# Dispatching sixteen experts from GpSimd: unrolled, with indices read in place, four output buffers and gathers five experts ahead

## The chip, the cores and the metric

The kernel runs on one core of a Trainium2 chip. The time is the device time of one execution in microseconds (us). All runs shown are of one core, and the time is that of the whole program: two transformer layers, of which the change touches one stage.

## The reference

The input x is 2 x 1024 tokens of 128 numbers. Four blocks follow each other, each with a residual and a layer norm: an attention with its own scoring, a mixture of 16 experts, a softmax attention, and a mixture of 8 experts. The change lies in the second block. Cut to what matters there:

```python
E, D = 16, 128; I = 4 * D; C = int(T * 2.0 / E)           # T = 2048 tokens, so C = 256 an expert
logits = flat_x @ gate_w.T
scores = softmax(logits, axis=-1).T
topk_weight, topk_idx = top_k(scores, C)                  # each expert picks its 256 tokens
xg = flat_x[topk_idx]                                     # gather
g = einsum("ecd,eid->eci", xg, Wg); u = einsum("ecd,eid->eci", xg, Wu)
h = gelu(g) * u
eo = einsum("eci,edi->ecd", h, Wd) * topk_weight[..., None]
flat_out = zeros_like(flat_x).at[topk_idx.reshape(-1)].add(eo.reshape(-1, D))   # scatter-add
out = flat_out.reshape(b, s, d) + shared                  # shared: one dense gated layer for all tokens
```

A token can be picked by several experts, so scatters of different experts may add to the same row.

## The kernel before, in words

Each engine runs its own written-out list of instructions, and semaphores order them. Nothing is scheduled by a planner.

For the expert stage the token lists lie in the SBUF tile `idx` (128 partitions x 16 experts x 2 halves, NH = 2, so 256 tokens are two columns of 128). DRAM holds `xs_rows` (the tokens and their 16 scores, 144 numbers a row) and `moe_rows` (the output rows, already filled with residual and shared part). For each expert e = 4 * j + k:

- **GpSimd (POOL) gathers**: two indirect DMAs (L1967, one per half) copy the expert's 256 rows of `xs_rows` into `G[:, k]`. `G` has four buffers. Before this `gather` (L1963) copies the two index columns to `idx_in[:, k]`, and the DMAs read that copy.
- **TensorE (PE)** turns the tokens (L913), runs the two upward products (L925, `expert_up`) and the downward product (L935, `expert_down`) with weights that SyncE (SP) loads four experts ahead (`load_expert`, L569 and L570, issued as soon as the downward product of expert e is done, `down_full`).
- **ScalarE (ACT)** does the gelu (L1291). **VectorE (DVE)** copies the turned tokens to `GT` and increments `g_sb` (L1670), multiplies (L1677, `hidden`), and in `weigh` (L1685) writes the weighted output to `out_e[:, k % 2]`, of which there are two buffers, and increments `out_sb`. So it waits until the scatter of expert e - 2 has landed (`scattered`).
- **GpSimd scatters**: two indirect DMAs that add (L1983) from `out_e` to `moe_rows`, with an index copy of their own, `idx_out` (L1975). Since two scatters may meet on one row, scatter e waits until all of scatter e - 1 has landed (`scattered` at 32 * e), and until `out_sb` says e + 1.

GpSimd's list is in the order `ORDER`, once for experts 0 to 3, then in a loop over j = 1, 2 with register values in waits and indices, then the last four scatters:

```python
ORDER = [("g", 0), ("g", 1), ("s", 0), ("g", 2), ("s", 1), ("g", 3), ("s", 2), ("s", 3)]
```

"g", k gathers expert 4 * j + 4 + k. So between scatters 3 and 4 (7 and 8, and so on) lie two gathers, and none between 2 and 3 (6 and 7, 10 and 11). The tiny `carrier` addition (L1958, `carry_waits`) stands between the waits and the DMAs; it computes nothing that is used. `idx_ready` counts the index copies.

After the last scatter has landed SP loads `moe_rows` back into `Z` (L594) and the layer norm on DVE (L1528 and on) begins; everything later in the program follows from that. Ahead of the stage, GpSimd waits for the lists (`idx_sb`, written by DVE at L1658).

Of the kernel before, what the change touches and what calls it, by code (L numbers as in the profile page):

```python
# [28 lines left out]
F32 = mybir.dt.float32  # L29
BF16 = mybir.dt.bfloat16  # L30
F16 = mybir.dt.float16
I32 = mybir.dt.int32
U32 = mybir.dt.uint32
ALU = mybir.AluOpType
# [3 lines left out]
P = 128  # L38
# [102 lines left out]
E0 = 16  # L141
I0 = 4 * P
CAP = 2 * B * T // E0
NH = CAP // P
# [31 lines left out]
def build(nc, a, out):  # L176
    with ExitStack() as whole:
        def sem(name):
            return whole.enter_context(nc.semaphore(name))
# [4 lines left out]
        def sb(name, shape, dt, scope=whole):  # L184
            return scope.enter_context(nc.sbuf_tensor(name, shape, dt))
# [6 lines left out]
        xs_rows = dram("xs_rows", [B * T, XW], F32)  # L192
        moe_rows = dram("moe_rows", [B * T, P], F32)
# [8 lines left out]
        banks = [t[:, h * BANK:(h + 1) * BANK] for t in (causal_ps[0], causal_ps[1], tail_ps, acc_ps)  # L202
                 for h in range(2)]
# [10 lines left out]
        eps_ln = sb("eps_ln", [P, 1], F32)  # L214
# [120 lines left out]
        lists = sb("lists", [P, 2, 16], F32, M)  # L335
        turned_l = sb("turned_l", [P, 2, 2, 16, 8], F32, M)
        idx = sb("idx", [P, E0, NH], I32, M)
        carrier = sb("carrier", [P, 1], F32, M)
        idx_in = sb("idx_in", [P, 4, NH], I32, M)
        idx_out = sb("idx_out", [P, 4, NH], I32, M)  # L340
        G = sb("G", [P, 4, NH, XW], F32, M)
        w_tok = sb("w_tok", [P, 4, NH], F32, M)
        GT = sb("GT", [P, 2, CAP], F32, M)
# [2 lines left out]
        wd = sb("wd", [P, 4, I0], F32, M)  # L346
        act_e = sb("act_e", [P, 4, CAP], F32, M)
        hid_e = sb("hid_e", [P, 2, 4, CAP], F32, M)
        out_e = sb("out_e", [P, 2, NH, P], F32, M)
        M.close()  # L350

        N = ExitStack()
# [85 lines left out]
        hid_done = sem("hid_done")  # L438
        down_full = sem("down_full")
        out_sb = sem("out_sb")  # L440
        idx_ready = sem("idx_ready")
        scattered = sem("scattered")
        z_in = [sem(f"z_in{n}") for n in range(CH)]
        w2_in = sem("w2_in")
# [913 lines left out]
        def _(dve):  # L1358
# [320 lines left out]

            def weigh(j, k):  # L1680
                dve.wait_ge(down_full, 4 * j + k + 1)
                if k >= 2 or not isinstance(j, int) or j > 0:
                    dve.wait_ge(scattered, 16 * NH * (4 * j + k - 1))
                for h in range(NH):
                    ins = dve.tensor_scalar(out_e[:, k % 2, h, :], banks[6 + k % 2][:, h * P:(h + 1) * P],  # L1685
                                            w_tok[:, k, h:h + 1], None, ALU.mult)
                ins.then_inc(out_sb, 1)

# [168 lines left out]
        def _(pool):  # L1857
# [95 lines left out]
            pool.wait_ge(masks_ready, 3)  # L1953
            pool.nop().then_inc(masks_ready, 1)

            def carry_waits():

                pool.tensor_tensor(carrier[:, :], eps_ln[:, :], eps_ln[:, :], ALU.add)  # L1958

            def gather(e, k):  # L1960

                src = idx[:, e, :] if isinstance(e, int) else idx[:, bass.ds(e, 1), :].rearrange("p o h -> p (o h)")
                pool.tensor_copy(idx_in[:, k, :], src).then_inc(idx_ready, 1)  # L1963

            def fetch(k):
                for h in range(NH):
                    pool.indirect_dma_start(out=G[:, k, h, :], out_offset=None, in_=xs_rows,  # L1967
                                            in_offset=bass.IndirectOffsetOnAxis(ap=idx_in[:, k, h:h + 1].bitcast(U32), axis=0)
                                            ).then_inc(gathered[k], 16)

            def scatter(j, k):

                e = 4 * j + k
                src = idx[:, e, :] if isinstance(e, int) else idx[:, bass.ds(e, 1), :].rearrange("p o h -> p (o h)")
                pool.tensor_copy(idx_out[:, k, :], src).then_inc(idx_ready, 1)  # L1975
                pool.wait_ge(idx_ready, 4 + (8 * j if not isinstance(j, int) or j < 3 else 24) + scat_at(j, k))
                pool.wait_ge(out_sb, e + 1)

                if not (isinstance(e, int) and e == 0):
                    pool.wait_ge(scattered, 16 * NH * e)  # L1980
                carry_waits()
                for h in range(NH):
                    pool.indirect_dma_start(out=moe_rows, in_=out_e[:, k % 2, h, :], in_offset=None,  # L1983
                                            out_offset=bass.IndirectOffsetOnAxis(ap=idx_out[:, k, h:h + 1].bitcast(U32), axis=0),
                                            compute_op=ALU.add).then_inc(scattered, 16)

            ORDER = [("g", 0), ("g", 1), ("s", 0), ("g", 2), ("s", 1), ("g", 3), ("s", 2), ("s", 3)]

            def scat_at(j, k):

                order = ORDER if not isinstance(j, int) or j < 3 else [o for o in ORDER if o[0] == "s"]
                return order.index(("s", k)) + 1

            pool.wait_ge(idx_sb, 1)
            pool.wait_ge(xs_out, 16 * 2)
            for k in range(4):
                gather(k, k)
            pool.wait_ge(idx_ready, 4)  # L2000
            for k in range(4):
                fetch(k)
            pool.wait_ge(sh_out, 16 * CH)

            def four_experts(j):
                for n, (kind, k) in enumerate(ORDER):
                    if kind == "g":

                        pool.wait_ge(g_sb, 4 * j + k + 1)
                        gather(4 * j + 4 + k, k)  # L2010
                        pool.wait_ge(idx_ready, 4 + 8 * j + n + 1)
                        carry_waits()
                        fetch(k)
                    else:
                        scatter(j, k)

            four_experts(0)
            with pool.Fori(1, E0 // 4 - 1) as j:
                four_experts(j)
            for k in range(4):  # L2020
                scatter(E0 // 4 - 1, k)


            pool.wait_ge(w2_in, 16 * 6)
# [94 lines left out]
```

## Time and profile before

| | us |
|---|---|
| median of 3 runs | 1172.78 |
| lowest, highest of them | 1169.59, 1176.74 |
| the profiled execution's own time | 1178.61 |
| its span | 1176.9 |
| granted TensorE clock, mean over the span | 0.875 of full |
| busy PE, DVE, ACT, POOL | 987.0, 746.4, 556.4, 351.6 |

The span is the time between the first and last instruction that the profiler recorded. Busy shares are averages over stages with different limits: POOL is busy only 30% of the span, and still it can set the pace of one stage. Times in the trace are us from the start of the span. A view called chain of waits follows the work that ended last back in time; "issue" there is time in which an engine waited for nothing that the profile shows. A GpSimd DMA's recorded duration (DMA_INDIRECT) is the time in which the engine makes it up and issues it; its data lands later, and the landing shows as the end of a wait on it by another instruction.

### The profile page before, as it was taken

To read this page: it belongs to the slowest core of one execution; us is meant where nothing else is said; L and a number is where in the kernel's file an instruction comes from. 1 tells how busy PE (TensorE), PEld (TensorE's weight loads), DVE (VectorE), ACT (ScalarE), POOL (GpSimd) and SP (SyncE) were. 2 spreads that over 40 slices of the span, in tenths; PEclk is the share of its full clock that TensorE was granted. 3 is DMA by queue.
4 is the path that set the end of the run, shared out by engine and by line. 5 is a ranking of instruction groups with operands and counts; after the bars stand their busy time and mean duration, and the time that the engine had idled before them with its cause. 6 is when DMAs were issued, how large, how long until landed. Compare 5 with 4: busy or idle time off the path is not lost.

```text
span 1176.9 us, 18267 instructions
## 1 busy us (share of the span) xinstructions
PE 987.0 (84%) x6011; PEld 479.5 (41%) x6011; DVE 746.4 (63%) x1543; ACT 556.4 (47%) x607; POOL 351.6 (30%) x785
## 2 busy tenths in 40 slices
PE   5699999999999675398745788999999887999996
PEld 3222222223222543387742433333333226566664
DVE  5778788787887566443224895777877305644446
ACT  2578778777777321222213304555555773222222
POOL 3043343443344400267751202333333440000000
PEclk8599799998988778599986556999999997999998
DMA  4401101101100302056522422221121100000001
GB/s 129 143 1 41 41 1 40 40 1 39 40 1 1 122 9 67 15 137 151 142 25 63 170 83 82 83 64 62 47 77 42 43 1 28 14 14 27 13 13 36
DMA packets 45655, 63.27 MB, mean 54 GB/s; under 512 B 7720, under 2 KB 33672, under 8 KB 42120
## 3 DMA queue, kind: packets, MB, share of 16 engines
q1 hardware_dynamic: 39968, 58.11, 15.8%
q0 software_dynamic: 5632, 4.46, 2.6%
q8 instruction: 31, 0.51, 0.2%
q14 instruction: 24, 0.20, 0.1%
HBM read 50.69 MB, written 11.86 MB: 53 GB/s over the span
## 4 chain that ended last, share of the span: by engine, by line
PE 53%; DVE 21%; issue 10%; POOL 6%; ACT 5%; DMA 4%; DVEq 0%; SPq 0%; POOLq 0%; ACTq 0%
PE acc_ps L748 10%; PE causal_ps L1135 9%; DVE mx L498 6%; PE acc_ps L1042 6%; PE tail_ps L988 5%; PE tail_ps L1145 5%; PE causal_ps L1025 3%; DVE R L1424 3%; PE causal_ps L710 3%; POOL moe_rows L1983 2%; DMA moe_rows<-out_e,idx_out 2%; DVE tails L1430 2%; PE causal_ps L721 2%; ACT EX L1312 2%; POOL G L1967 2%
## 5 line engine op out<-in xcount | busy, mean ns | idle before, releaser
L1312 ACT ACTIVATE EX<-causal_ps 128x1024 f32<-128x1024 f32 (+1 forms) x160 | 146.8, 938 | 157.0 <-PE causal_ps L1025 155.9
L498 DVE TENSOR_REDUCE mx<-tail_ps 128x1 f32<-128x512 f32 x266 | 157.6, 632 | 41.2 <-PE tail_ps L991 22.7
L1205 ACT ACTIVATE R<-R 128x2048 f32<-128x2048 f32 (+1 forms) x80 | 135.3, 1731 | 2.0 <-DVE R L1424 1.9
L1135 PE MATMUL causal_ps<-XT,w 128*128 128x512 f32 x256 | 117.4, 606 | 2.6 <-DVE hid_f L1802 1.9
L1424 DVE TENSOR_SCALAR R<-causal_ps 128x1024 f32<-128x1024 f32 (+1 forms) x96 | 102.5, 1082 | 17.2 <-PE causal_ps L710 16.7
L988 PE MATMUL tail_ps<-KM,QM 72*128 72x512 bf16 (+1 forms) x320 | 105.1, 357 | 8.7 <-DVE mx L498 3.0
L1025 PE MATMUL causal_ps<-QE,KE 75*128 75x512 bf16 (+3 forms) x384 | 102.6, 338 | 8.5 <-ACT EX L1312 3.1
L1430 DVE TENSOR_REDUCE tails<-causal_ps 128x1 f32<-128x768 f32 (+5 forms) x88 | 89.6, 1019 | 25.4 <-PE causal_ps L721 24.8
L1348 ACT ACTIVATE act_f<-causal_ps 128x512 f32<-128x512 f32 x64 | 38.2, 597 | 130.1 <-PE causal_ps L1135 130.1
L1212 ACT ACTIVATE R<-R 128x1792 f32<-128x1792 f32 (+4 forms) x80 | 96.9, 1263 | 0.0
L748 PE MATMUL acc_ps<-R,sum_sel 128*32 128x512 f32 (+3 forms) x768 | 88.2, 534 | 6.6 <-ACT Ysb L1218 6.6
L2043 POOL TENSOR_TENSOR pacer<-eps_ln 128x1 f32<-128x1 f32 x160 | 30.9, 193 | 208.4 <-ACT EX L1312 207.7
L1900 POOL TENSOR_TENSOR R<-R 128x512 f32<-128x512 f32 (+2 forms) x64 | 87.0, 1375 | 1.3
L748 PE MATMUL acc_ps<-R,VS 128*32 128x512 f32 (+3 forms) x768 | 84.6, 538 | 0.5 <-POOL R L1900 0.5
L1802 DVE TENSOR_TENSOR hid_f<-act_f,causal_ps 128x512 f32<-128x512 f32 x64 | 43.9, 687 | 64.1 <-ACT act_f L1348 64.0
L1042 PE MATMUL acc_ps<-EX,VS 128*32 128x512 f32 (+3 forms) x768 | 82.9, 507 | 0.6 <-POOL EX L2046 0.6
L710 PE MATMUL causal_ps<-QS,KS 72*128 72x512 bf16 (+3 forms) x288 | 71.1, 356 | 14.6 <-DVE tails L1430 7.3
L1892 POOL TENSOR_TENSOR holder<-eps_ln 128x1 f32<-128x1 f32 x40 | 7.7, 193 | 222.5 <-ACT R L1205 222.5
L2046 POOL TENSOR_SCALAR_AFFINE_SELECT EX<-EX 128x128 f32<-128x128 f32 x256 | 70.8, 292 | 0.0
L1135 PEld LDWEIGHTS causal_ps<-XT,w 128*128 128x128 f32 x256 | 47.1, 194 | 55.8 <-issue 44.1
L988 PEld LDWEIGHTS tail_ps<-KM,QM 72*128 72x128 bf16 x320 | 31.5, 101 | 85.1 <-DVE mx L498 71.2
L1145 PEld LDWEIGHTS tail_ps<-w,hid_f 128*128 128x128 f32 x512 | 60.9, 192 | 11.5 <-issue 11.5
(266 smaller groups left out, 1604.9 us busy)
## 6 DMA issues: line engine op xcount, KB each, us to landing
QS<-q_parts SPq DMA_DIRECT2D x8, 576.0 KB
KS<-k_parts SPq DMA_DIRECT2D x24, 192.0 KB
QM<-q_parts SPq DMA_DIRECT2D x8, 576.0 KB
KM<-k_parts SPq DMA_DIRECT2D x24, 192.0 KB
QE<-q_parts SPq DMA_DIRECT2D x8, 576.0 KB
KE<-k_parts SPq DMA_DIRECT2D x24, 192.0 KB
wg<-in_wg_t SPq DMA_DIRECT2D x16, 256.0 KB
wu<-in_wu_t SPq DMA_DIRECT2D x16, 256.0 KB
```

Source lines behind the costliest of these rows:

```text
L498: return reduce(mx[:, par, hh, o0:o0 + step * (cnt - 1) + 1:step], scores[:, 0:cnt * w].rearrange("p (c w) -> p c w", w=w), AX.X, op, **how)
L710: mm = pe.matmul(slot[:, c0:c1], KS[0:ROWS, par, hh, kt * P:(kt + 1) * P], QS[0:ROWS, par, hh, q0:q0 + c1 - c0], start=True, stop=True)
L748: mm = pe.matmul(acc_ps[hh * VW:(hh + 1) * VW, qa:qb], w, src[:, rp, hh, c0:c0 + qb - qa], start=(kt == 0 and not powered), stop=last, til ...
L988: mm = pe.matmul(slot[:, at:at + w], QM[0:ROWS, par, hh, i * P:(i + 1) * P], KM[0:ROWS, par, hh, k0:k0 + w], start=True, stop=not diag, sk ...
L1025: mm = pe.matmul(causal_ps[hh % 2][:, c0:c1], KE[0:MROWS, par, hh, kt * P:(kt + 1) * P], QE[0:MROWS, par, hh, q0:q0 + c1 - c0], start=True ...
L1042: mm = pe.matmul(acc_ps[hh * VW:(hh + 1) * VW, qa:qb], VS[:, par, kt, hh * VW:(hh + 1) * VW], EX[:, rp, hh, c0:c0 + qb - qa], start=(kt == 0),
L1135: mm = pe.matmul(banks[2 * ring + o], w[:, k, m * P:(m + 1) * P], XT[:, n * BANK:(n + 1) * BANK], start=True, stop=True)
L1145: mm = pe.matmul(banks[4 + n % 2][:, i * P:(i + 1) * P], hid_f[:, n % 2, m, i * P:(i + 1) * P], w2[:, k, m, :], start=(m == 0), stop=(m == ...
L1205: act.activation(R4[:, rp, h0:h0 + 2, 0:width], R1[:, rp, h0:h0 + 2, 0:width], ACT.Square).then_inc(squared, 1)
L1312: act.activation(EX[:, rp, hh, 0:width], causal_ps[hh % 2][:, 0:width], ACT.Exp, scale=float(D) ** -0.5).then_inc(exp_done, 1)
L1424: return dve.tensor_scalar(R1[:, rp, hh, 0:width], slot[:, 0:width], 0.0, None, ALU.max)
L1430: return dve.tensor_reduce(tails[:, par, i, h0:h0 + per], slot[:, 0:per * stride].rearrange("p (h w) -> p h w", w=stride)[:, :, 0:w], AX.X ...
```

## The change

On GpSimd the copies `idx_in` and `idx_out`, the semaphore `idx_ready`, the `carrier` additions and the loop are gone. The indirect DMAs read `idx` itself, and all sixteen experts are written out, with constants in waits and addresses. The order becomes: gathers 0 to 3 and 4, then for each expert e gather e + 5 (while there is one) and scatter e. `out_e` has four buffers in place of two, so `weigh` of expert e waits for scatter e - 4. All other engines keep their lists. `G` keeps its four buffers: gather e + 5 waits for `g_sb` at e + 2, which is the copy of the tokens of expert e + 1. Scatter e still waits for all of scatter e - 1.

```diff
-        out_e = sb("out_e", [P, 2, NH, P], F32, M)
+        out_e = sb("out_e", [P, 4, NH, P], F32, M)
...
-                if k >= 2 or not isinstance(j, int) or j > 0:
-                    dve.wait_ge(scattered, 16 * NH * (4 * j + k - 1))
+                if not isinstance(j, int) or j > 0:
+                    dve.wait_ge(scattered, 16 * NH * (4 * j + k - 3))
...
-                    ins = dve.tensor_scalar(out_e[:, k % 2, h, :], banks[6 + k % 2][:, h * P:(h + 1) * P],
+                    ins = dve.tensor_scalar(out_e[:, k, h, :], banks[6 + k % 2][:, h * P:(h + 1) * P],
...
+            def gather(e):
+                if e >= 4:
+                    pool.wait_ge(g_sb, e - 3)
                 for h in range(NH):
+                    pool.indirect_dma_start(out=G[:, e % 4, h, :], out_offset=None, in_=xs_rows,
+                                            in_offset=bass.IndirectOffsetOnAxis(ap=idx[:, e, h:h + 1].bitcast(U32), axis=0)
+                                            ).then_inc(gathered[e % 4], 16)
+
+            def scatter(e):
                 pool.wait_ge(out_sb, e + 1)
+                if e:
                     pool.wait_ge(scattered, 16 * NH * e)
-                carry_waits()
                 for h in range(NH):
+                    pool.indirect_dma_start(out=moe_rows, in_=out_e[:, e % 4, h, :], in_offset=None,
+                                            out_offset=bass.IndirectOffsetOnAxis(ap=idx[:, e, h:h + 1].bitcast(U32), axis=0),
                                             compute_op=ALU.add).then_inc(scattered, 16)
...
-            for k in range(4):
-                gather(k, k)
-            pool.wait_ge(idx_ready, 4)
-            for k in range(4):
-                fetch(k)
+            for e in range(4):
+                gather(e)
             pool.wait_ge(sh_out, 16 * CH)
...
-            four_experts(0)
-            with pool.Fori(1, E0 // 4 - 1) as j:
-                four_experts(j)
-            for k in range(4):
-                scatter(E0 // 4 - 1, k)
+            gather(4)
+            for e in range(E0):
+                if e + 5 < E0:
+                    gather(e + 5)
+                scatter(e)
```

GpSimd's list, at one iteration of the loop before: from the gather between scatters 4 and 5 to scatter 5 (`ISA` and `REGISTER_ALU` rows compute register values; a row with x2 is one DMA for each half).

```order
L1963 ISA [waits g_sb]
L1963 COPY idx_in<-idx 128x2
L2011 REGISTER_ALU
L1958 TENSOR_TENSOR carrier<-eps_ln 128x1 [waits idx_ready]
L1967 DMA G<-xs_rows,idx_in 128x144 x2
L1975 ISA
L1975 COPY idx_out<-idx 128x2
L1976 REGISTER_ALU
L1980 REGISTER_ALU [waits out_sb,idx_ready]
L1958 TENSOR_TENSOR carrier<-eps_ln 128x1 [waits scattered]
L1983 DMA moe_rows<-out_e,idx_out 2048x128 x2
```

The same piece of GpSimd's list in the changed kernel, one gather and one scatter, as it recurs ten times:

```order
L1956 DMA G<-xs_rows,idx 128x144 [waits g_sb]
L1956 DMA G<-xs_rows,idx 128x144
L1965 DMA moe_rows<-out_e,idx 2048x128 [waits scattered,out_sb]
L1965 DMA moe_rows<-out_e,idx 2048x128
```

The four DMAs are the same in size; two copies, two carriers and the register rows between them are gone, and the waits stand on the first DMA of each pair.

The place between scatters 2 and 4, from the list before (the fixed part for experts 0 to 3; behind the branch the loop begins with two gathers):

```order
L1983 DMA moe_rows<-out_e,idx_out 2048x128 x2
L1975 COPY idx_out<-idx 128x2
L1958 TENSOR_TENSOR carrier<-eps_ln 128x1 [waits scattered,out_sb,idx_ready]
L1983 DMA moe_rows<-out_e,idx_out 2048x128 x2
L2018 UNCONDITIONAL_BRANCH
```

In the changed kernel each of scatters 1 to 10 has one gather ahead of it, this place included, so gathers 8 and 12 have moved ahead of scatters 3 and 7. Scatters 11 to 15 have none, as 12 to 15 had none before.

## Rows read from the trace of the kernel before

**Rows 1.** Chain of waits, 490 to 626 us: shares of that stretch by line.
```profile
by line: issue 25.0%; POOL moe_rows L1983 21.3%; DMA moe_rows<-out_e,idx_out 19.0%; POOL G L1967 14.1%; PE causal_ps L925 4.2%; PE tail_ps L925 3.2%; POOL carrier L1958 2.8%; DMA Z<-moe_rows 2.1%; DMA G<-xs_rows,idx_in 1.9%; POOL idx_in L19
```
**Rows 2.** Waits, 490 to 625 us: us in total, times, longest.
```profile
POOL carrier L1958 <- DMA moe_rows<-out_e,idx_out: 13.5, 8, 2.1
DVE out_e L1685 <- DMA moe_rows<-out_e,idx_out: 50.8, 12, 7.5
```
**Rows 3.** Timeline, POOL: start us, us, operation, count, idle before.
```profile
489.94 0.55 POOL L1963 COPY idx_in<-idx 128x2 int32<-128x2 int32 x4 [82.24 <-DVE idx L1658]
490.79 1.20 POOL L1967 DMA_INDIRECT G<-xs_rows,idx_in  x1 [0.30 <-POOL idx_in L1963]
...
510.06 0.19 POOL L1958 TENSOR_TENSOR carrier<-eps_ln 128x1 f32<-128x1 f32 x1 [3.43 <-DVE out_e L1685]
510.75 1.64 POOL L1983 DMA_INDIRECT moe_rows<-out_e,idx_out  x1 [0.50 <-issue]
```
**Rows 4.** Timeline, POOL, scatter 5, gather 10, scatter 6.
```profile
550.45 1.63 POOL L1983 DMA_INDIRECT moe_rows<-out_e,idx_out  x1 [0.48 <-issue]
552.38 1.59 POOL L1983 DMA_INDIRECT moe_rows<-out_e,idx_out  x1 [0.30 <-issue]
...
554.25 0.19 POOL L1958 TENSOR_TENSOR carrier<-eps_ln 128x1 f32<-128x1 f32 x1
554.59 1.03 POOL L1967 DMA_INDIRECT G<-xs_rows,idx_in  x1
555.93 0.98 POOL L1967 DMA_INDIRECT G<-xs_rows,idx_in  x1 [0.30 <-issue]
...
557.94 1.63 POOL L1983 DMA_INDIRECT moe_rows<-out_e,idx_out  x1 [0.48 <-issue]
```
**Rows 5.** Timeline, POOL: scatter 10, then the last scatters, 14 and 15.
```profile
589.08 1.64 POOL L1983 DMA_INDIRECT moe_rows<-out_e,idx_out  x1 [0.48 <-issue]
...
614.50 1.55 POOL L1983 DMA_INDIRECT moe_rows<-out_e,idx_out  x1 [0.30 <-issue]
...
617.88 0.19 POOL L1958 TENSOR_TENSOR carrier<-eps_ln 128x1 f32<-128x1 f32 x1 [1.64 <-DMA moe_rows<-out_e,idx_out]
618.51 1.55 POOL L1983 DMA_INDIRECT moe_rows<-out_e,idx_out  x1 [0.44 <-issue]
```
**Rows 6.** Timeline, POOL: second half of scatter 1, and the wait for its landing.
```profile
519.77 1.57 POOL L1983 DMA_INDIRECT moe_rows<-out_e,idx_out  x1 [0.31 <-issue]
...
525.60 0.19 POOL L1958 TENSOR_TENSOR carrier<-eps_ln 128x1 f32<-128x1 f32 x1 [1.13 <-DMA moe_rows<-out_e,idx_out]
```
**Rows 7.** Timeline, POOL: second halves of scatters 2, 4 and 8.
```profile
528.20 1.58 POOL L1983 DMA_INDIRECT moe_rows<-out_e,idx_out  x1 [0.30 <-issue]
...
544.91 1.57 POOL L1983 DMA_INDIRECT moe_rows<-out_e,idx_out  x1 [0.30 <-issue]
...
576.07 1.56 POOL L1983 DMA_INDIRECT moe_rows<-out_e,idx_out  x1 [0.30 <-issue]
```
**Rows 8.** Timeline, DVE: `weigh` 4, 6, 7, 10, released by scatters 2, 4, 5, 8.
```profile
531.97 0.61 DVE L1685 TENSOR_SCALAR out_e<-acc_ps,w_tok 128x128 f32<-128x128 f32 x2 [1.11 <-DMA moe_rows<-out_e,idx_out]
...
549.51 0.61 DVE L1685 TENSOR_SCALAR out_e<-acc_ps,w_tok 128x128 f32<-128x128 f32 x2 [6.31 <-DMA moe_rows<-out_e,idx_out]
...
555.71 0.61 DVE L1685 TENSOR_SCALAR out_e<-acc_ps,w_tok 128x128 f32<-128x128 f32 x2 [3.78 <-DMA moe_rows<-out_e,idx_out]
...
580.79 0.61 DVE L1685 TENSOR_SCALAR out_e<-acc_ps,w_tok 128x128 f32<-128x128 f32 x2 [7.53 <-DMA moe_rows<-out_e,idx_out]
```
**Rows 9.** By stretch: us, busy PE, PEld, DVE, ACT, POOL, clock, DMA share, GB/s.
```profile
510.00:542.00 32.00, 30.50 (x185) 27.46 (x183) 15.07 (x44) 9.20 (x24) 23.65 (x32) 1.00 0.72 179
542.00:592.00 50.00, 40.23 (x233) 36.03 (x234) 14.66 (x50) 9.96 (x26) 38.72 (x52) 0.97 0.55 132
```
**Rows 10.** Timeline, PE: upward product's start, experts 4 and 5; tokens 6 turned.
```profile
520.50 0.60 PE L925 MATMUL causal_ps<-GT,wg 128*128 128x256 f32 x2
...
525.96 0.60 PE L925 MATMUL causal_ps<-GT,wg 128*128 128x256 f32 x2
...
529.41 0.38 PE L913 MATMUL causal_ps<-ident,G 128*128 128x128 f32 x2
```

More of the change, by code:

```diff
@@ L337, in build @@
         idx = sb("idx", [P, E0, NH], I32, M)
-        carrier = sb("carrier", [P, 1], F32, M)
-        idx_in = sb("idx_in", [P, 4, NH], I32, M)
-        idx_out = sb("idx_out", [P, 4, NH], I32, M)
         G = sb("G", [P, 4, NH, XW], F32, M)
@@ L440, in build @@
         out_sb = sem("out_sb")
-        idx_ready = sem("idx_ready")
         scattered = sem("scattered")
@@ L1954, in _ @@
             pool.nop().then_inc(masks_ready, 1)
[L1956 to L1965, printed above, removed]
-                for h in range(NH):
-                    pool.indirect_dma_start(out=G[:, k, h, :], out_offset=None, in_=xs_rows,
-                                            in_offset=bass.IndirectOffsetOnAxis(ap=idx_in[:, k, h:h + 1].bitcast(U32), axis=0)
-                                            ).then_inc(gathered[k], 16)
@@ L1971, in scatter @@
[L1971 to L1976, printed above, removed]
+            def gather(e):
+                if e >= 4:
+                    pool.wait_ge(g_sb, e - 3)
+                for h in range(NH):
+                    pool.indirect_dma_start(out=G[:, e % 4, h, :], out_offset=None, in_=xs_rows,
+                                            in_offset=bass.IndirectOffsetOnAxis(ap=idx[:, e, h:h + 1].bitcast(U32), axis=0)
+                                            ).then_inc(gathered[e % 4], 16)
@@ L1977, in scatter @@
+            def scatter(e):
                 pool.wait_ge(out_sb, e + 1)
-                if not (isinstance(e, int) and e == 0):
+                if e:
                     pool.wait_ge(scattered, 16 * NH * e)
-                carry_waits()
                 for h in range(NH):
-                    pool.indirect_dma_start(out=moe_rows, in_=out_e[:, k % 2, h, :], in_offset=None,
-                                            out_offset=bass.IndirectOffsetOnAxis(ap=idx_out[:, k, h:h + 1].bitcast(U32), axis=0),
+                    pool.indirect_dma_start(out=moe_rows, in_=out_e[:, e % 4, h, :], in_offset=None,
+                                            out_offset=bass.IndirectOffsetOnAxis(ap=idx[:, e, h:h + 1].bitcast(U32), axis=0),
@@ L1985, in scatter @@
                                             compute_op=ALU.add).then_inc(scattered, 16)
[L1989 to L1994, printed above, removed]
             pool.wait_ge(idx_sb, 1)
             pool.wait_ge(xs_out, 16 * 2)
-            for k in range(4):
-                gather(k, k)
@@ L2000, in _ @@
-            pool.wait_ge(idx_ready, 4)
-            for k in range(4):
-                fetch(k)
-            pool.wait_ge(sh_out, 16 * CH)
[L2005 to L2015, printed above, removed]
```

## The prediction

> **What bounds the kernel now.** The change touches one stage, so I read first the chain of waits over that stage, then who waits for whom, then GpSimd's timeline, since the chain runs on GpSimd. The reader should see in the chain [rows 1] that scatters (21.3%), their landings (19.0%), gathers (14.1%), carriers and the gaps called "issue" make up most of these 136 us, while the upward products of TensorE have 7.4%. So the stage lasts as long as GpSimd's list, from the first scatter at 510.75 [rows 3] to the last at 618.51 [rows 5]: 107.76 us for 15 steps. The largest wait of the stage is a trap: VectorE waits 50.8 us for `out_e` buffers, GpSimd only 13.5 us for landings [rows 2]. VectorE's wait is the effect of a slow GpSimd: TensorE, where nothing held it, took 525.96 - 520.50 = 5.46 us an expert [rows 10], while GpSimd takes 557.94 - 550.45 = 7.49 [rows 4]. Freeing VectorE alone gives nothing at the end of the stage.
>
> **A step of GpSimd, taken apart.** From scatter 5 to scatter 6 [rows 4]: the scatter pair 552.38 + 1.59 - 550.45 = 3.52; to the gather 0.62 (end of the index copy, carrier, gaps); the gather pair 555.93 + 0.98 - 554.59 = 2.32; to the next scatter 557.94 - 556.91 = 1.03 (copy, carrier, a gap of 0.48). Sum 7.49.
>
> **Start of the stage.** Four copies and a gap, 490.79 - 489.94 = 0.85, stand ahead of the first gather [rows 3]. They go; a gap before the DMA stays, and I take the 0.30 of that row: 0.55 earlier. All of it is on the path, since that gather leads to the first tokens and the first output. At the first scatter there were 0.19 of carrier and 0.50 of gap behind the wait [rows 3]. The carrier goes, and of the gap I keep the 0.44 of rows 5: 0.25 earlier. So scatter 0 starts at 510.75 - 0.80 = 509.95.
>
> **Scatters 0 to 10**, ten steps with one gather each. The two DMA pairs stay, 3.52 + 2.32 = 5.84. What stands ahead of a DMA with a satisfied wait and nothing to carry it, the trace doesn't show. Below it is bounded by the gap behind the carrier of a gather (554.59 - 554.44 = 0.15), above by the 0.48 behind that of a scatter [rows 4]. I take 0.30, the gap between the two DMAs of a pair, the nearest row to one DMA right behind another. Step: 5.84 + 0.60 = 6.44, with ends at 6.14 and 6.80. Ten are 64.4; before they were 589.08 - 510.75 = 78.33 [rows 3, 5]. The 13.9 us between them hold two things: the copies, carriers and register work (1.05 a step), and the places between scatters 2 and 3 and between 6 and 7, where no gather covered the landing.
>
> **Late landings.** Scatter e waits for the landing of scatter e - 1, and a DMA behind a wait that has held it starts some 0.44 after its release [rows 5]. So the cover of 0.30 + 2.32 + 0.30 = 2.92 us is enough for a landing of up to 2.48. Scatter 1 was issued by 521.34 and released its waiter at 525.60: 4.26 [rows 6]. Scatters 4 and 8 were issued by 546.48 and 577.63 and released VectorE at 549.51 and 580.79: 3.0 and 3.2; scatters 2 and 5 took 2.2 and 1.7 [rows 4, 7, 8], and the four others up to scatter 9 lie between these two. The three late ones are over by 1.8, 0.5 and 0.7: 3.0 in nine landings, 0.33 a step, 3.3 in ten. By those of the loaded stretch alone, 1 to 4, it is 2.3 in four, 5.8 in ten. TensorE no longer waits, so the weight loads that share the DMA engines keep for all ten steps the pace of 510 to 542 us, with a share of 0.72 where the next stretch had 0.55 [rows 9]. I take 4.5, between the two. Ten steps: 68.9.
>
> **The rule that speaks against this.** The landings spread from 1.7 to 4.3 us in one stage [rows 6 to 8], and most are at the short end. The Trainium skill, page DMA: Bandwidth & Descriptors, section Latency and other measured facts, says that the access time of the device memory goes from 0.2 us on average to 2 us at high load, and that this is the main part of a transfer's fixed cost. By an estimate from that page every landing of the ten would be 1.8 us above a quiet one. This trace agrees with the size of the spread, not with every landing being late under load.
>
> **Scatters 10 to 15**, five steps without a gather (before, these had none either). The last one [rows 5]: the pair 3.41, then from 616.05 to the carrier's start at 617.88 1.83, carrier 0.19, gap 0.44, sum 5.87. Without the carrier, and with its gap kept, 5.68; if the gap shrinks to 0.30, 5.54. I take 5.68, in all 28.4, against 618.51 - 589.08 = 29.43 before. The weight loads end before this stretch in both.
>
> **What costs nothing.** Four `out_e` buffers: at TensorE's free pace expert e is weighed near 510 + 5.5 e, and scatter e - 4 has landed by 509.95 + 6.9 (e - 4) + 5.5, which is the later one only from e = 16 on. So VectorE never waits there. Gathers: gather 6 is issued by 516.1 and lands 2 to 3 us later, 10 us ahead of its use at 529.41 [rows 10]. It loses 1.4 us an expert, so by the last gather the slack is spent and TensorE may wait a few us. What covers that: scatter 15 begins over 10 us after TensorE is done. The gathers' waits on `g_sb` are for tokens that VectorE has copied before it weighs the expert that the scatter behind them waits for, so they hold nothing up. SP and its queue keep their order. The reload of `Z` and all that follows move up as a block, at the clock of before, as TensorE stands idle some 25 us ahead of them in both.
>
> **Sum.** Last scatter at 509.95 + 68.9 + 28.4 = 607.25, against 618.51: 11.3 us earlier. The profiled execution, 1178.6, would become 1167.3. It lies 5.8 above the median of the runs, 1172.8; I apply the difference to the median: 1161.5.
>
> **Rivals.**
> - *The waits on the DMAs cost what the carriers cost*, so the change doesn't do what it says. For it: even behind a carrier the DMA came 0.44 to 0.50 later where a wait had held it [rows 3, 5]. Against: 0.15 where none had [rows 4]. The step then keeps 0.62 + 1.03: ten are 74.9, 3.4 less than before, and 0.5 at the start; time 1168.9. Chance 0.09.
> - *No landing is late and the gaps are short.* Step 6.14, five steps of 5.54: 3.0 + 0.7 + 4.5 less than my forecast, 1153.3. For it: six of nine landings at 1.7 to 2.2. Chance 0.17.
> - *Every landing is late by what load adds.* The three late landings (3.0, 3.2, 4.26 [rows 6 to 8]) have a mean of 3.5, against the quiet 1.83 of rows 5; I take 3.6. Then GpSimd waits ahead of each of scatters 1 to 10, 3.6 + 0.44 - 2.92 = 1.12 a step, 11.2 in place of 4.5: 1168.2, or 1172 at 4.0. For it: the share of 0.72 now lasts. Against: scatter 2, in that very stretch. This is also what the skill's page would give. Chance 0.12.
> - *The landing becomes slower than all that was removed* (the other side). The wait on `scattered` in front of scatters 1 to 10 makes a step 3.52 + landing + 0.44. It decides from a landing of 4.06 on: ten steps of 8.02 (78.33, and the 0.8 and 1.05 saved elsewhere) give the time of before. At scatter 1's 4.26 all along it is 1174.8, and each further us of landing adds 10: at 5.3 it is 1185. For it: rows 6, and a TensorE that no longer pauses its loads. Against: one such landing in nine. Chance 0.05.
>
> **How the numbers follow.** My forecast has 0.57, with 1157 to 1166 as its own range (gap 0.15 to 0.48, late landings 0 to 6 us). About 0.5% (5.9 us) is what a measurement of this kernel can tell from no change, so faster means below 1166.9. The range 1151 to 1169 takes in the short gaps and the nearer half of the two cases near 1168, and leaves out 0.2. Faster: 0.57 + 0.17, and a part of those two, 0.79. Same 0.16. Slower 0.05.
>
> **What would show it.** GpSimd has no copy and no carrier in the stage. From one scatter to the next it takes 6.4 us with a gather between, more where a landing is late, and 5.7 for the last five. VectorE's wait for scatters is gone, the weight loads come every 5.5 us to the last, and GpSimd's waits for landings stand mostly at scatters 11 to 15. The later stages are as long as before. Wrong would be steps over 7 us: if the idle time ahead of scatters is put down to the landings of `moe_rows`, load did it; if to "issue", the waits.

## The result, and the profile after

The changed kernel takes 1159.73 us (median of 5 runs, 1157.05 to 1163.31), against 1173.74 for the kernel before in the runs beside it (5 runs, 1169.59 to 1176.74). The ratio is 0.9892, with a 95% interval of 0.986 to 0.9923, which is 9 to 16 us. By the ratio the kernel is 12.7 us faster, by the difference of the two medians 14.0, where 11.3 were forecast. The profiled execution took 1157.05 us with a span of 1155.3; that is 21.6 less than the span of before, more than the ratio says. Some 7 us of it lie ahead of the stage and 2 behind it. The 7 are in code that the change does not touch: the index lists are written at 489.88 us before and at 482.63 after, and over all traces of this study between 480.7 and 491.8. So the stage is measured below from that point, and not from the start of the span.

From the lists to the first statistics of the layer norm behind the stage it was 626.45 - 489.88 = 136.6 us before. Now it is 607.07 - 482.63 = 124.4. That is 12.1 us less, nearly all of the gain.

GpSimd's timeline from the lists to scatter 4 (start us, us, operation, count, and in brackets the idle time before it and what ended it):

```profile
482.93 1.20 POOL L1956 DMA_INDIRECT G<-xs_rows,idx  x1 [81.27 <-DVE idx L1654]
...
502.27 1.65 POOL L1965 DMA_INDIRECT moe_rows<-out_e,idx  x1 [4.33 <-DVE out_e L1681]
504.22 1.57 POOL L1965 DMA_INDIRECT moe_rows<-out_e,idx  x1 [0.30 <-issue]
506.10 1.01 POOL L1956 DMA_INDIRECT G<-xs_rows,idx  x1 [0.30 <-issue]
507.42 0.98 POOL L1956 DMA_INDIRECT G<-xs_rows,idx  x1 [0.30 <-issue]
508.71 1.63 POOL L1965 DMA_INDIRECT moe_rows<-out_e,idx  x1 [0.30 <-issue]
...
523.65 1.59 POOL L1965 DMA_INDIRECT moe_rows<-out_e,idx  x1 [0.30 <-issue]
525.54 1.01 POOL L1956 DMA_INDIRECT G<-xs_rows,idx  x1 [0.30 <-issue]
526.87 0.97 POOL L1956 DMA_INDIRECT G<-xs_rows,idx  x1 [0.30 <-issue]
529.52 1.63 POOL L1965 DMA_INDIRECT moe_rows<-out_e,idx  x1 [1.68 <-DMA moe_rows<-out_e,idx]
```

Where no landing is late, the plain gap of 0.30 stands between any two pairs of DMAs, and a step is 508.71 - 502.27 = 6.44 us, where [rows 4] had 7.49. The last row is a scatter held by a late landing: a step of 7.80. The end of the list, scatters 10, 11, 14 and 15, against [rows 5]:

```profile
569.71 1.63 POOL L1965 DMA_INDIRECT moe_rows<-out_e,idx  x1 [0.30 <-issue]
571.64 1.59 POOL L1965 DMA_INDIRECT moe_rows<-out_e,idx  x1 [0.30 <-issue]
575.67 1.57 POOL L1965 DMA_INDIRECT moe_rows<-out_e,idx  x1 [2.45 <-DMA moe_rows<-out_e,idx]
...
593.31 1.55 POOL L1965 DMA_INDIRECT moe_rows<-out_e,idx  x1 [2.45 <-DMA moe_rows<-out_e,idx]
...
599.19 1.55 POOL L1965 DMA_INDIRECT moe_rows<-out_e,idx  x1 [2.47 <-DMA moe_rows<-out_e,idx]
```

Without copy or carrier the last steps are 599.19 - 593.31 = 5.88, to the hundredth what they were. Who waited for whom in the stage, against [rows 2] (us in total, times, longest):

```profile
POOL moe_rows L1965 <- DMA moe_rows<-out_e,idx: 13.2, 6, 2.5
DVE out_e L1681 <- DMA moe_rows<-out_e,idx: 4.4, 4, 1.5
PE causal_ps L909 <- DMA G<-xs_rows,idx: 0.5, 1, 0.5
```

VectorE's wait has gone from 50.8 to 4.4 us, GpSimd's own from 13.5 to 13.2 only. (The prediction had VectorE never wait: its last output did wait 1.5 us for scatter 11 to land, which cost nothing.) The stretches (us, busy PE, PEld, DVE, ACT, POOL, clock, DMA share, GB/s), against [rows 9], and the chain of waits over 490 to 626 us, against [rows 1]:

```profile
510.00:542.00 32.00, 32.00 (x202) 29.33 (x201) 15.74 (x47) 8.90 (x24) 24.55 (x20) 1.00 0.75 183
542.00:592.00 50.00, 38.05 (x243) 34.61 (x242) 18.80 (x55) 11.43 (x28) 33.55 (x25) 0.93 0.52 111
```
```profile
by line: PE causal_ps L921 17.5%; PE tail_ps L921 16.7%; PE acc_ps L931 15.8%; DMA moe_rows<-out_e,idx 14.5%; issue 7.9%; POOL moe_rows L1965 6.9%; PE causal_ps L909 2.1%; DMA Z<-moe_rows 2.0%; PE causal_ps L957 2.0%; DVE stats L1524 1.8%; 
```

A warning on this chain: it now goes over TensorE, and yet TensorE is not what sets the end. It changes engines at gather 15:

```profile
567.11 1.01 POOL L1956 DMA_INDIRECT G<-xs_rows,idx  x1 [0.30 <-DVE GT L1666]
```

The profile names VectorE's copy of tokens that ended just before, at 566.9, which are those of expert 14. But this gather waits for `g_sb` at 12, the copy for expert 11, which began some 17 us earlier, and its idle time is the plain 0.30. So it waited for nobody. TensorE in turn waited 0.5 us, once, for a gather: its lead over GpSimd is used up by the last tokens, as the prediction had it.

The table gives this section's measures for all traces, each of one execution: from scatter 0 to 10 (ten steps, ten gathers between), from 10 to 15 (five steps, none between), and from the lists to the layer norm's first statistics.

| kernel | 0 to 10 | 10 to 15 | lists to norm | ratio to before |
|---|---|---|---|---|
| before | 78.33 | 29.43 | 136.6 | 1 |
| changed | 67.44 | 29.48 | 124.4 | 0.9892 (0.986 to 0.9923) |
| before, four buffers | 78.20 | 30.38 | 137.2 | 0.9988 (0.9957 to 1.0018) |
| changed, two buffers | 67.89 | 29.65 | 125.2 | 0.9876 (0.9835 to 0.9918) |
| changed, waits swapped | 65.80 | 27.17 | 121.5 | 0.9855 (0.9814 to 0.9896) |
| changed, no weight loads | 64.83 | 29.60 | 122.2 | 0.9863 (0.9794 to 0.9933) |
| before, loop written out | 78.21 | 29.82 | 136.7 | 0.9997 (0.9962 to 1.0032) |
| changed, old order | 74.26 | 29.41 | 131.5 | 0.9916 (0.9884 to 0.9949) |
| changed, with copies and carriers | 71.87 | 30.59 | 131.0 | 0.9948 (0.9916 to 0.998) |
| changed, two destinations | 64.37 | 18.72 | 113.8 to the first addition | 0.9793 (0.9729 to 0.9857) |
| changed, loads after landings | 65.22 | 30.44 | 123.2 | 0.9865 (0.9814 to 0.9917) |
| changed, both of those | 64.36 | 29.21 | 121.1 | 0.9849 (0.9795 to 0.9903) |

The intervals of the ratios are some 3.5 to 8 us to either side. They tell the large edits apart; for the small ones the stage's own times are what is read, and these are single executions in which the landings vary by a us or two.

### The profile page after: what moved, and what is told of

It is laid out like the page before. It is cut to its first block, busy times and chain, and to the rows that moved or that the text cites. A ratio compares the mean times of both kernels' runs of the same rounds, so it can differ in the third digit from the quotient of the medians.

```text
span 1155.3 us, 18154 instructions
## 1 busy us (share of the span) xinstructions
PE 972.6 (84%) x6011; PEld 471.1 (41%) x6011; DVE 748.0 (65%) x1543; ACT 556.5 (48%) x607; POOL 340.4 (29%) x725
## 4 chain that ended last, share of the span: by engine, by line
PE 59%; DVE 22%; issue 8%; ACT 5%; DMA 3%; POOL 2%; DVEq 0%; SPq 0%; ACTq 0%; POOLq 0%
PE causal_ps L1131 10%; PE acc_ps L744 9%; DVE mx L494 6%; PE acc_ps L1038 6%; PE tail_ps L984 5%; PE tail_ps L1141 5%; PE causal_ps L1021 3%; DVE R L1420 3%; PE causal_ps L706 3%; PE causal_ps L921 2%; PE tail_ps L921 2%; PE acc_ps L931 2%; DVE tails L1426 2%; PE causal_ps L717 2%; ACT EX L1308 2%
## 5 line engine op out<-in xcount | busy, mean ns | idle before, releaser
L1208 ACT ACTIVATE R<-R 128x1792 f32<-128x1792 f32 (+4 forms) x80 | 96.9, 1263 | 0.0
L1798 DVE TENSOR_TENSOR hid_f<-act_f,causal_ps 128x512 f32<-128x512 f32 x64 | 43.9, 687 | 64.3 <-ACT act_f L1344 64.2
L744 PE MATMUL acc_ps<-R,VS 128*32 128x512 f32 (+3 forms) x768 | 79.2, 509 | 0.9 <-POOL R L1896 0.9
```

The source lines that it names most:

```text
L744: mm = pe.matmul(acc_ps[hh * VW:(hh + 1) * VW, qa:qb], w, src[:, rp, hh, c0:c0 + qb - qa], start=(kt == 0 and not powered), stop=last, til ...
```

## The experiments

### Which part of the change brought the gain: the buffers

```diff
-        out_e = sb("out_e", [P, 2, NH, P], F32, M)
+        out_e = sb("out_e", [P, 4, NH, P], F32, M)
...
-                if k >= 2 or not isinstance(j, int) or j > 0:
-                    dve.wait_ge(scattered, 16 * NH * (4 * j + k - 1))
+                if not isinstance(j, int) or j > 0:
+                    dve.wait_ge(scattered, 16 * NH * (4 * j + k - 3))
```

on the kernel before (with `k` for `k % 2` in the two uses of `out_e`).

> The kernel before with four output buffers instead of two, nothing else. Theory (GpSimd's list sets the stage, VectorE's 50.8 us of waiting is an effect): VectorE's wait for scatters nearly goes, but from scatter 0 to scatter 15 it is 107.8 us as before, give or take 2, and the ratio to the kernel before is 1.000. Rival (the buffers were what the change gained by): scatter 0 to 15 near 97 us as in the changed kernel, ratio near 0.99.

Measured: 78.20 us for ten steps against 78.33, and a ratio of 0.9988. The wait that stood out most in the profile of before is gone:

```profile
DVE out_e L1685 <- DMA moe_rows<-out_e,idx_out: 4.5, 3, 2.7
DVE out_e L1685 <- PE acc_ps L935: 12.2, 12, 2.7
```

46 us of waiting were taken from VectorE, and the stage did not become shorter. The converse, the same edit backwards in the changed kernel (two buffers, `e % 2`):

> The changed kernel with two output buffers instead of four. Theory: scatter 0 to 15 stays at 96.9 us within 2 us, TensorE and VectorE are held at GpSimd's pace and weight loads come less densely, so landings are late less often: it may be 1 to 3 us shorter. Ratio to the kernel before 0.985 to 0.99. Rival (the buffers matter): it falls back by several us towards 107.

Measured: 67.89 against 67.44, the lists to the norm 125.2 against 124.4, ratio 0.9876. Nothing lost, and nothing gained either: that landings would be late less often did not come true. Seven of ten scatters started late, by 0.2 to 0.8 us and 3.6 in all (the DMA share in 510 to 542 us is 0.75 with two buffers as with four). The rival is out. The buffers are worth nothing here.

### The loop, the copies and the order

```diff
             four_experts(0)
-            with pool.Fori(1, E0 // 4 - 1) as j:
+            for j in range(1, E0 // 4 - 1):
                 four_experts(j)
```

> The kernel before with GpSimd's loop over experts written out, so that waits and indices are constants; copies, carriers, order and buffers as before. Theory: the eight steps of the loop lose the gap that register work makes (0.48 to 0.15 ahead of a scatter's DMA, 0.16 ahead of its carrier), about 0.45 a step, so scatter 0 to 10 falls from 78.3 to about 75; ratio 0.997. Rival: the loop is the whole price, near 67.

Measured: 78.21 against 78.33, ratio 0.9997. The single steps did become shorter, 7.08 where the loop had 7.48 (scatter 9 to 10 in both), but the sum did not. The traces show where it went. The carrier ahead of scatter 7, which has no gather to cover the landing of scatter 6, before:

```profile
563.54 0.19 POOL L1958 TENSOR_TENSOR carrier<-eps_ln 128x1 f32<-128x1 f32 x1 [1.87 <-DMA moe_rows<-out_e,idx_out]
```

and with the loop written out:

```profile
554.73 0.19 POOL L1958 TENSOR_TENSOR carrier<-eps_ln 128x1 f32<-128x1 f32 x1 [3.50 <-DMA moe_rows<-out_e,idx_out]
```

The landing came 1.6 us later and ate what four steps had saved. In all, six steps lost 0.4 us each; the landings took back 1.9 ahead of scatter 7 and 1.2 ahead of scatters 5 and 9, and gave 1.0 ahead of scatter 2. So the rival, the loop as the whole price, is out. That it is worth nothing is not shown: the register work does cost 0.4 us a step, the sum of one execution hides it behind its landings, and the ratio that was expected, 0.997, lies inside the interval. Now the order, put back into the changed kernel:

```diff
-            gather(4)
             for e in range(E0):
-                if e + 5 < E0:
-                    gather(e + 5)
+                for g in {0: (4, 5), 1: (6,), 2: (7,), 3: ()}[e % 4]:
+                    if e < E0 - 4:
+                        gather(e // 4 * 4 + g)
                 scatter(e)
```

> The changed kernel with the gathers in the order of before (two between scatters 3 and 4, none between 2 and 3, and so on). Theory: the two scatters without a gather ahead are held by landings (5.9 instead of 3.8 each), while the double gathers cover late landings: scatter 0 to 10 is 2 to 5 us longer than 67.4. Rival: the order is worth nothing, as each late landing that it makes it also hides: 67 to 68.

Measured: 74.26 us, 6.8 more than the changed kernel; from the lists to the norm 7.1 more. More than I expected. The two scatters without a gather ahead, 3 and 7:

```profile
531.84 1.55 POOL L1965 DMA_INDIRECT moe_rows<-out_e,idx  x1 [3.82 <-DMA moe_rows<-out_e,idx]
...
561.43 1.57 POOL L1965 DMA_INDIRECT moe_rows<-out_e,idx  x1 [3.68 <-DMA moe_rows<-out_e,idx]
```

They wait 3.8 and 3.7 us, where the same gap is 2.4 to 2.6 in the quiet last steps: under weight loads an uncovered landing takes over a us longer, and both are paid in full. Moving two gathers by one place covers them. Scatters 2, 6, 9 and 10 started late too in this trace, by 0.5 to 1.5 us beyond the plain gap, where only two did by over 0.2 us in the changed kernel: 3.5 us of lateness in all against 3.1, so nearly all of the 6.8 us is the two uncovered landings. Last the copies and carriers, in the changed kernel, written out:

```diff
+            def copy_index(dst, e):
+                pool.tensor_copy(dst, idx[:, e, :]).then_inc(idx_ready, 1)
+                copies[0] += 1
+                pool.wait_ge(idx_ready, copies[0])
...
             def gather(e):
                 if e >= 4:
                     pool.wait_ge(g_sb, e - 3)
+                copy_index(idx_in[:, e % 4, :], e)
+                carry_waits()
...
             def scatter(e):
+                copy_index(idx_out[:, e % 4, :], e)
                 pool.wait_ge(out_sb, e + 1)
                 if e:
                     pool.wait_ge(scattered, 16 * NH * e)
+                carry_waits()
```

> The changed kernel with the index copies and the carriers put back in front of each gather and scatter, written out with constants. Theory: 0.62 us stand ahead of each pair instead of 0.30, so the steps with a gather are 7.1 us instead of 6.4: scatter 0 to 10 near 71, less what the longer cover saves in late landings; the last five steps stay at 5.9, as the copy and carrier run under the landing. Rival: the carriers hide the DMA's own start and cost nothing: 67.

Measured: steps of 7.09 to 7.11, as expected, with two late ones (7.71 and 7.38) among them; 71.87 for ten, 4.4 more. The last five are 30.59, of which 6.78 is one late landing and the others 5.90 to 6.00: there the carrier costs at most 0.1 us. So by the traces, of the 10.9 us by which ten steps became shorter, the order has 6 to 7 and the copies and carriers 4 to 4.5. Over the whole stretch from the lists to the norm they are nearly equal, 7.1 us and 6.6: the copies also cost 0.8 us ahead of scatter 0, and that trace has a late landing behind scatter 10.

The times of the whole program do not bear out that the order is the larger part. Both kernels ran ten times side by side: the old order's median is 1164.43 us, that with copies and carriers 1170.01, so there the copies cost 5.6 us more. By the ratios the old order gives up 2.8 us of the gain, the copies 6.6, though the intervals (0.9884 to 0.9949, and 0.9916 to 0.998) overlap. The trace of the old order is also of the slowest of its ten executions, 1175.25 us. That both parts count is shown by the rows; which is the larger is open.

### The landings: late because of the weight loads, or of themselves

```diff
-            with sp.Fori(0, E0 // 4 - 1) as j:
-                for k in range(4):
-
-                    sp.wait_ge(down_full, 4 * j + k + 1)
-                    load_expert(4 * j + 4 + k, k)
...
-                pe.wait_ge(weights[k], 16 * 3 * (j + 1))
+                pe.wait_ge(weights[k], 16 * 3)
```

> The changed kernel without the weight loads of experts 4 to 15 (the weights of experts 0 to 3 are used again; this part of the result is another). Theory of late landings: with quiet DMA engines no scatter among 1 to 10 is held by a landing, the ten steps take 64.3 us instead of 67.4, and the last five stay at 5.9. Rival (landings are late of themselves, as in scatters 4 and 9): 67 us again, with the same two or three late ones.

Measured (this kernel leaves the loads out and returns another result): the stretch's DMA share falls from 0.75 to 0.32 (us, busy PE, PEld, DVE, ACT, POOL, clock, DMA share, GB/s):

```profile
508.00:540.00 32.00, 32.00 (x202) 29.34 (x201) 15.59 (x46) 9.20 (x24) 25.73 (x20) 1.00 0.32 43
```

and the ten steps take 64.83 us. Nine of them are 6.43 to 6.45. One, of 6.91, had a late landing all the same, 0.5 us beyond the cover. So nearly all of the 3.1 us of lateness comes from the loads, as the theory had it.

What in the loads? In the changed kernel SP issued the three loads for one expert at these times (the third of each, at the scatters that were late and at one that was not):

```profile
502.39 0.38 SPq L566 DMA_DIRECT2D wd<-in_wd_t  x1
...
524.73 0.38 SPq L566 DMA_DIRECT2D wd<-in_wd_t  x1
...
552.04 0.38 SPq L566 DMA_DIRECT2D wd<-in_wd_t  x1
```

Scatters 3 and 7, the late ones, were issued by 523.65 + 1.59 = 525.24 and by 552.59, both about 0.5 us behind such a load. Scatter 0 was issued by 505.79, 3.4 us behind one, and was in time; so, within 0.2 us, were all others, at 2.8 us or more behind a load or just ahead of one. That led to this experiment:

```diff
-            with sp.Fori(0, E0 // 4 - 1) as j:
-                for k in range(4):
-
-                    sp.wait_ge(down_full, 4 * j + k + 1)
-                    load_expert(4 * j + 4 + k, k)
+            for e in range(E0 - 4):
+                sp.wait_ge(down_full, e + 1)
+                if e:
+                    sp.wait_ge(scattered, 16 * NH * e)
+                load_expert(e + 4, e % 4)
```

> The changed kernel, with the weight loads of expert e + 4 held until scatter e - 1 has landed (as well as until the downward product of e is done, as now). The bytes are the same, only their place against the scatters is fixed. Theory: in the changed kernel the two late landings (of scatters 3 and 7) belong to the two scatters that were issued within 1.5 us behind a weight load; TensorE's 5.46 us and GpSimd's 6.4 us drift past each other, so it happens about every fourth step. With the loads issued right at a landing none is late: steps of 6.43, ten in 64.3 us (now 67.4), the last five at 5.9. Rival (it is the amount of traffic, not its place): two or more late landings as before, 66 to 69 us.

Measured: 65.22 us. Nine steps of 6.43 to 6.46, and one of 7.27, though that scatter (1) was issued 3.6 us behind a load. Scatter 11 landed 0.7 us late as well. So the place of the loads makes most late landings, but not each of them: the rule is a tendency, and what made scatter 1 late here is open. Scatter 11 was the one nearest to its loads: the landing of scatter 10 releases both it and the last set of loads, and no gather stands between. It was issued 4.1 us behind the set's first load, where scatters 2 to 10 of this trace had 4.2 to 4.7. In the total it can't be told from the changed kernel (0.9865 against 0.9892).

All traces together say more. In the six that have these waits and a cover of 2.9 us (changed, two buffers, waits swapped, old order, loads after landings, both of those), 18 scatters were fully issued within 3.1 us after the first load of a set of three had begun, so while a set was being issued or shortly behind it. Of these 17 held up the next scatter, by 0.2 to 1.4 us. The 38 others were issued 3.5 us or more behind a set's first load, and only two of them were late by over 0.3 us.

### Where the wait stands

The trace's own records show where each of a scatter's two waits went: the one written last, for the landing, became an instruction of its own ahead of the DMA, and only the one written first, for the output, rides on the DMA (the list printed with the change puts both at the DMA). The experiment exchanges them:

```diff
             def scatter(e):
-                pool.wait_ge(out_sb, e + 1)
                 if e:
                     pool.wait_ge(scattered, 16 * NH * e)
+                pool.wait_ge(out_sb, e + 1)
```

> The changed kernel with the two waits of a scatter in the other order, so that the wait for the landing stands on the DMA itself and the one for the output ahead of it. In the changed kernel a DMA held by a landing began 0.63 to 0.69 us after it, the one held by an output (scatter 0) 0.28 after. Theory: what is late is the DMA behind a wait that has no instruction to ride on, so the steps of scatters 10 to 15 fall from 5.9 to 5.5 us, 2 us in all. Rival: the time from a landing to the next scatter is the landing's own, and the steps stay at 5.87.

Measured: 27.17 us for the last five steps against 29.48, 65.80 for ten against 67.44. The same two scatters at the end, now with waits of 2.0 us where it was 2.45:

```profile
594.31 1.55 POOL L1965 DMA_INDIRECT moe_rows<-out_e,idx  x1 [1.98 <-DMA moe_rows<-out_e,idx]
...
599.70 1.55 POOL L1965 DMA_INDIRECT moe_rows<-out_e,idx  x1 [1.98 <-DMA moe_rows<-out_e,idx]
```

A DMA that carries its held wait starts 0.46 us sooner behind it than one whose wait is an instruction ahead. The recorded increments of `scattered` say the same. From the landing to the start of the next scatter it is 0.73 us in the changed kernel's last five steps and 0.27 with the waits exchanged. The landing itself takes 1.7 to 1.8 us behind the issue in both. From the lists to the norm it is 121.5 us, 2.9 less than the changed kernel; the ratio, 0.9855, agrees but can't show so little. Both small edits together:

> Both edits at once, the swapped waits and the loads held until a landing, in one destination. If the two are independent: ten steps in 64.3 to 64.8 us and five in 27.2, so 91.5 to 92 us from scatter 0 to scatter 15 against 96.9 in the changed kernel and 83.1 with two destinations; about 1155. Rival: the loads that are held come late for TensorE, which then holds scatters up in the second half, and steps grow over 7 us there.

Measured: ten steps in 64.36 us, all of 6.42 to 6.45, and five in 29.21, since scatter 11's landing came late (a step of 7.18 where its neighbours have 5.4 to 5.6); here too the last set of loads was released together with it, 3.6 us ahead of the end of its issue. In all 93.6 against the 91.5 to 92 expected. TensorE's waits for weights rose from none to 3.2 us and held nothing up. The median, 1160.7 in a spread of 1150 to 1166, says nothing between these versions.

### A version without the wait: two destinations

```diff
+        moe_second = dram("moe_second", [B * T, P], F32)
...
+                if e >= 2:
+                    pool.wait_ge(scattered[e % 2], 16 * NH * (e // 2))
+                elif e == 1:
+                    pool.wait_ge(second_set, 16)
+                pool.wait_ge(out_sb, e + 1)
                 for h in range(NH):
+                    pool.indirect_dma_start(out=(moe_rows, moe_second)[e % 2], in_=out_e[:, e % 4, h, :], in_offset=None,
...
+            def both(n):
+                dve.wait_ge(z_in[n], 16 * 2)
+                part = slice(n * CT, (n + 1) * CT)
+                dve.tensor_tensor(Z[:, part, :], Z[:, part, :], YF[:, part, :], ALU.add).then_inc(z_sum, 1)
+                dve.wait_ge(z_sum, n + 1)
```

The second destination is filled with zeros from `Y` while GpSimd is idle ahead of the stage, and comes back into `Y`, which is free there.

> The changed kernel with two destinations in device memory: even experts add into the first (with the residual), odd ones into a second that was filled with zeros, and VectorE adds both behind the stage. So scatter e waits for the landing of e - 2 only. Theory: no scatter is held by a landing; ten steps at 6.43 and five at 3.8 make 83.5 us instead of 96.9. Behind it the second reload and four additions cost about 3 us. In all 9 to 11 us faster than the changed kernel, near 1149 to 1151. Rival: two scatters in flight hold each other up in the DMA engines, the last steps stay above 5 us and the gain is under 5.

Measured: 83.09 us from scatter 0 to 15, where 83.5 was expected. The list has no wait for a landing at all:

```profile
POOL moe_second L1984 <- issue: 4.9, 16, 0.3
POOL moe_rows L1984 <- issue: 4.6, 15, 0.3
POOL moe_rows L1984 <- DVE out_e L1690: 4.3, 1, 4.3
```

```profile
571.40 1.63 POOL L1984 DMA_INDIRECT moe_rows<-out_e,idx  x1 [0.30 <-issue]
573.34 1.59 POOL L1984 DMA_INDIRECT moe_rows<-out_e,idx  x1 [0.30 <-issue]
575.23 1.57 POOL L1984 DMA_INDIRECT moe_second<-out_e,idx  x1 [0.30 <-issue]
```

It is the fastest kernel of the study: 1152.99 us (4 runs), ratio 0.9793 (0.9729 to 0.9857). The 9 to 11 us that I expected against the changed kernel can't be checked closely, as the two ran beside different runs of the kernel before: the medians differ by 6.7 us, by 8.7 when each is taken against its own runs of before (22.7 less and 14.0 less), and the ratios by 11.6. The traces can be added up. The stage gave its share: 13.8 us less from scatter 0 to 15. Scatter 0 came 1.0 us later behind the lists in this trace (20.6 against 19.6). The second reload, issued once the last scatter has landed, brought its first part at 600.26, 6.7 us behind the last scatter's issue, against 4.5 for one destination: 2.3 us. It is the last landing that was late: 4.0 us behind the issue, by the recorded increments, where the five before it took 1.65 to 1.70. The four DMAs of the first reload had been issued from 591.48 on and were under way beside it; that they made it late is likely and not tested. The additions stand on the path of the layer norm, which takes 12.1 us in place of 9.3:

```profile
600.26 0.69 DVE L1717 TENSOR_TENSOR Z<-Z,Y 128x512 f32<-128x512 f32 x1 [15.49 <-DMA Y<-moe_second]
600.98 0.87 DVE L1533 BATCH_NORM_STATS2 stats<-Z 128x6 f32<-128x128 f32 x4
```

That leaves 13.8 - 1.0 - 2.3 - 2.8 = 7.7 us by the traces, somewhat less than expected, and inside what the runs allow.

## Why the prediction was right, and where its terms were not

**The bound.** GpSimd's list sets the stage, and VectorE's 50.8 us of waiting were an effect: shown, by four buffers in the kernel before (no change) and two in the changed one (none either).

**The start.** Forecast 0.80 us earlier at scatter 0, measured 1.23 from the lists (20.87 to 19.64). The first gather began 0.30 behind the lists, as taken, and not 0.91: 0.61 for the 0.55 of the sum. At scatter 0 the DMA started 0.28 behind the end of the output (501.99 to 502.27), not 0.14 and 0.44: the gap was taken from a case where the wait does not ride on the DMA.

**The gap.** 0.30 was chosen between 0.15 and 0.48, and it is 0.30 between all pairs that no landing held up. A step is 6.43 us where 6.44 stood.

**Late landings.** Forecast 4.5 us in ten steps, measured 67.44 - 64.3 = 3.1: two of ten over the cover by 1.4 each, three by 0.13 to 0.17. Between the bounds of 0 and 6; the choice was too high by 1.4. The cover was reckoned as good for a landing of 2.48, with 0.44 from release to start; with the 0.73 to 0.77 measured it is good for 2.2 only, and three landings of 2.26 to 2.30 were just over it. The reason given, that loads make them, is borne out by the trace without loads, where 0.5 us of lateness was left. The rule of the Trainium skill (page DMA: Bandwidth & Descriptors, section Latency and other measured facts) that was weighed against it would have made every landing late and the time near 1168; at a DMA share of 0.75 (510 to 542 us) and after it, eight of ten stayed under or within 0.2 us of the cover, and five of them landed 1.6 to 1.7 us behind their issue, no later than the quiet ones at the end. An uncovered landing under load did grow, by 1.2 to 1.4 us (3.8 and 3.7 against 2.4 to 2.6, old order), which agrees with that rule's direction.

**The last five steps.** This term failed: 28.4 forecast, 29.48 measured, and 29.43 before. I took the carrier's 0.19 off and kept its gap. But 2.46 us stood between the end of a scatter and the next with and without the carrier. From the landing to the DMA's start it was 0.80 us with the carrier and 0.73 without, so its removal gave 0.07 and not 0.19. Even that is hidden in the sum, as the landings of the last three steps were 0.05 us longer in this trace and the step from 10 to 11 had been short before (0.41 in place of 0.80). The landing's wait had no instruction to ride on, and most of what the carrier had taken became part of the DMA's own start. The exchange of the waits shows that it is the wait's place: 27.17.

**The sum.** Scatter 0 to 15 was forecast at 97.3 us (68.9 + 28.4) and took 96.9; 11.3 us of gain were forecast and 12.7 measured, within the interval. The errors of the terms (start 0.4, lateness 1.4, last steps -1.1) partly cancelled, so that the sum came this close is in part luck.

**What stood behind the step.** Of the 13.9 us of the ten steps I gave 1.05 a step to copies, carriers and register work, 10.5 in all, and the rest to the two uncovered landings. The sum over ten steps did not need the split, and by the traces the split was wrong: put back into the changed kernel, copies and carriers cost 4.4, the old order 6.8. Written out in the kernel before, the loop gave 0.4 in single steps and nothing in the sum of its one trace.

**The rivals.** Waits costing what carriers cost: no for gathers and scatters that are not held, nearly so for held ones, where removing the carrier gave 0.07. No late landing and short gaps: no, 0.30 held everywhere. All landings late, and landings above 4.06: no.

## What to carry to other kernels

Where an engine's list sets a stage and holds waits for its own transfers, put other work of the same list into each wait before shortening the instructions around it: here two gathers moved by one place gave about as much as all removed copies (7.1 and 6.6 us of the stage in the traces, in the other order by the medians). Look where a wait ends up in the built program: on the instruction that it holds it cost 0.27 us, as an instruction ahead of it 0.73. When a wait exists only because two transfers add into one place, a second place and one addition may be cheaper: it removed all of that waiting here, for 5 us behind the stage.

## What the runs showed that I had not expected

- A DMA on GpSimd whose held wait stands ahead as an instruction starts 0.46 us later than one that carries it (gap from scatter to scatter 2.45 to 2.48 against 1.94 to 2.06).
- Without a landing to wait for, scatters to two destinations go out every 3.7 us, back to back, and the landings of one do not hold up the other: those of scatters 10 to 14 came 1.65 to 1.70 us behind their issue. Only the last of all, beside the first reload, took 4.0.
- A scatter issued within 0.6 us behind 768 KB of weight loads landed 1.4 us late, one issued 2.8 us behind or more in most cases in time; over six traces, 17 of 18 issued within 3.1 us after the first load of a set were late, and two of 38 others. One landing was late without any load (0.5 us) and two at 3.6 and 3.9 us behind the last load (0.8 and 1.5 us); the cause of these is open.
- The chain of waits of a kernel whose two engines almost touch can change engines at a point where the idle time before the instruction is the ordinary gap: it is then no proof of what bounds it.
